# Sending the answers of the first eight expert tiles behind up to four later ones, in a routed two-layer kernel

## The chip, the core and the metric

One Trainium2 chip, one of its cores. The time is the device time of one execution in microseconds; of before there are three, and one more that was profiled. The engines are TensorE (PE), VectorE (DVE), ScalarE (ACT), GpSimd (POOL) and SyncE (SP); each works through its own instructions in order and waits for the others through semaphores.

## What is computed

Two layers over 8 x 256 tokens of width 128, each a mixing block and a feed-forward block, with a residual and a layer norm behind each. The change lies in the feed-forward block of the first layer, where each token goes to two of eight experts:

```python
scores = softmax(x2d @ gate_w.T, axis=1)
top_scores, sel = top_k(scores, 2)
# rows sorted by expert, scaled by their score
h = silu(xe @ w1[e]) * (xe @ w3[e])      # hidden width 352
out = out + h @ w2[e]                    # per expert e
out = zeros.at[token_idx].add(routed_out)
```

All of it is float32; large products are made of three passes over high and low parts.

## The kernel before

**Routing.** A first stage computes the mixing block, batch by batch. For each batch and each of its 4 columns of routed rows, GpSimd sends the rows (token, score and the place where the answer belongs) with an indirect DMA to `routed` in DRAM (`scatter`, L464 to L469), sorted by expert. The rows of batches 0 to 3 serve the first 9 expert tiles, those of 4 and 5 the next 6, the rest the last 24 (`PHASE_TILES`): 39 tiles of 128 rows (`SLOT_TILES`). The first 15 (`AHEAD`) start while the routing of the last batches still runs.

**Expert tiles.** Each tile t passes through these steps, and each engine works on several tiles at once, in a fixed order written out by hand:

- SyncE loads its 128 rows from `routed` (`load_rows`, L368 to L376), after the row transpose of tile t - 3.
- TensorE transposes them (`row_transpose`, L1782); ScalarE and VectorE make the high part (`high_row`, L740) and the low part (`low_row`, L1312).
- TensorE makes the two up products (`up_products`, L1784, matmuls at L1617 to L1619); ScalarE applies silu (`gate_row`, L746) and VectorE multiplies (`gated_row`, L1321).
- TensorE turns the hidden rows (L1806), VectorE copies them (`turned_row`, L1328), TensorE makes the down product (L1817).
- ScalarE copies the result into the tile's row buffer and counts `mo["out"]` up by one (`answer`, L752).
- GpSimd sends it with an indirect DMA of 128 rows to `answers` in DRAM (`store_answers`, L562 to L568). Where a DMA is sent by GpSimd, the instruction on GpSimd computes its descriptors and the DMA engines move the data later.

In step t ScalarE does `high_row(t)`, `gate_row(t - 1)`, `answer(t - 4)`. VectorE and TensorE have similar steps.

**Buffers.** The rows of tiles 0 to 14 have a place of their own each (`rows_ahead`), which no other tile takes. Tiles from 15 on share a ring of 11.

**GpSimd's order.** Its last scatters (batches 6 and 7) are followed at once by `store_answers(0)`, `store_answers(1)` and so on; from tile 14 on one piece of weight preparation follows each store (`prepare`, splits into high and low parts), and from tile 31 on attention work of the second layer is mixed in. The loop is:

```python
for t in range(31):
    store_answers(t)
    if t >= AHEAD - 1:
        prepare(t - AHEAD + 1)
```

**SyncE's order.** Row loads of tiles 0 to 14, among them eight writes of padding rows into `routed` (`pads`, L382); `ff_out`; 1 MB of hidden weights (`ff_h[0]`, L397); row loads from tile 15 on; between those of tile 23 and 24 a wait for `mo["stored_ahead"]` (all stores of tiles 0 to 14) and the second 1 MB (L411, L412); in the end the answers by token (`load_answers`, L405), behind waits for the stores of the later tiles.

Of the kernel before, what the change touches and what calls it, by code (L numbers as in the profile page):

```python
# [81 lines left out]
def alone(engine, carrier):  # L82

    engine.sem_inc(carrier, 1)
# [7 lines left out]
def wait(engine, semaphore, value):  # L92

    if not isinstance(value, int) or value > 0:
        engine.wait_ge(semaphore, value)

def build(nc, A, out):
# [5 lines left out]
    with ctx:  # L104
# [3 lines left out]
        def sems(prefix, names):  # L108
            return {n: ctx.enter_context(nc.semaphore(f"{prefix}_{n}")) for n in names.split()}
# [136 lines left out]
        def routed_row(t):  # L246
            return rows_ahead[:, t, :] if t < AHEAD else rows_in[:, (t - AHEAD) % RING, :]
# [73 lines left out]
        mo = sems("mo", "tr hi lo up act1 hid hid_tr hidT down out stored_ahead")  # L321
# [118 lines left out]
        def _(pool):  # L440
# [119 lines left out]
                    split_bout(n - 7)  # L560

            def store_answers(t):  # L562
                pool.wait_ge(mo["out"], t + 1)
                wait(pool, mo_out[t % FLY], 16 * ((t - AHEAD) // FLY))
                alone(pool, carrier["pool"])
                nc.gpsimd.indirect_dma_start(  # L566
                    answers[:, :], bass.IndirectOffsetOnAxis(ap=routed_row(t)[:, AT_DEST:AT_DEST + 1].bitcast(u32), axis=0),
                    routed_row(t)[:, 0:D], None).then_inc(mo["stored_ahead"] if t < AHEAD else mo_out[t % FLY], 16)  # L568
# [47 lines left out]
# [4 lines that stand above are left out]
            def attention_first():  # L620
                store_answers(31)
                answers_sum(0)
                store_answers(32)
                answers_sum(1)
                x2_root(0)
                store_answers(33)
                store_answers(34)
                x2_root(1)
                low_x2(0)
                store_answers(35)  # L630
                answers_sum(2)
                pool.wait_ge(wt["ff_lo"], 2 * FF_TILES)
                pool.memset(own_column, 0.0).then_inc(at["ones"], 1)
                pool.wait_ge(at["ones"], 1)
                for c in range(GROUP_HEADS):
                    last = pool.memset(own_column[:, c, c * HEAD_DIM:(c + 1) * HEAD_DIM], 1.0)
                last.then_inc(at["ones"], 1)
                store_answers(36)
                low_parts(0, 0)
                store_answers(37)  # L640
                low_x2(1)
                store_answers(38)
                low_parts(0, 1)
                x2_root(2)
                answers_sum(3)
                low_parts(1, 0)
                low_x2(2)
                x2_root(3)
                answers_sum(4)
# [1586 lines left out]
```

## Time and profile before

| | |
|---|---|
| median of 3 runs | 369.46 us (369.4 to 369.9) |
| the profiled execution's own time | 370.72 us |
| its span, first to last instruction | 368.9 us |
| TensorE busy | 323.3 us, 88% |
| GpSimd busy | 173.4 us, 47% |
| mean granted TensorE clock | 0.96 of full speed |
| indirect stores of answers | 39, the first at 110.2 us, the last at 200.9 us |

Times in the views below are microseconds from the span's start, taken from the profiled execution. "Clock" is the share of TensorE's full clock (2.4 GHz) that was granted; 0.50 is 1.2 GHz.

### The profile page before, as it was taken

The page shows a single profiled execution, that of the slowest core. Times are in us where ns is not written, and L with a number is a line of the kernel's source. Part 1 is how long each engine was busy: PE and PEld are TensorE (multiplying, and loading weights), DVE is VectorE, ACT ScalarE, POOL GpSimd, SP SyncE. Part 2 cuts the span into 40 slices and gives each one's busy share as a digit, 9 for nine tenths or more (in the row PEclk, how much of TensorE's full clock was granted, in tenths as well). Part 3 has the DMA queues.
Part 4 walks back from the last instruction along what each step waited for, and adds up shares of the span by engine and source line. Part 5 has one row for each costly group of instructions (what it writes and reads, how often), then busy time and mean ns, then how long its engine had stood idle before and what let it go on. Part 6 is the DMA issues. An engine that isn't in the chain of part 4 may idle for free.

```text
span 368.9 us, 8839 instructions
## 1 busy us (share of the span) xinstructions
PE 323.3 (88%) x2692; PEld 295.2 (80%) x2692; DVE 261.1 (71%) x865; ACT 210.0 (57%) x430; POOL 173.4 (47%) x237
## 2 busy tenths in 40 slices
PE   3799999976777999999985989999798999999990
PEld 1789989866676999898975778888587999999990
DVE  3558988865873567769774699987796777677841
ACT  2354777635522355455438679898366668667330
POOL 1004677763464345886478677754211342244200
PEclk9999999987985999999999899999999999999997
DMA  8990011021132533421500300000000000000001
GB/s 274 431 367 1 16 37 40 29 61 29 43 97 59 186 85 92 140 60 53 165 23 29 115 2 2 3 3 0 3 3 0 2 16 16 14 14 0 16 14 32
DMA packets 17034, 23.73 MB, mean 64 GB/s; under 512 B 3424, under 2 KB 14176, under 8 KB 16208
## 3 DMA queue, kind: packets, MB, share of 16 engines
q1 hardware_dynamic: 13712, 17.97, 15.0%
q0 software_dynamic: 2272, 4.69, 3.9%
q10 hardware_dynamic: 1008, 0.53, 0.5%
q8 instruction: 23, 0.38, 0.4%
q14 instruction: 19, 0.16, 0.1%
HBM read 17.45 MB, written 6.73 MB: 66 GB/s over the span
## 4 chain that ended last, share of the span: by engine, by line
PE 44%; issue 12%; DVE 11%; POOL 9%; ACT 3%; POOLq 0%; DVEq 0%; ACTq 0%
PE ps L1985 8%; PE ps L1986 8%; PE ps L1817 6%; PE ps L1617 5%; POOL sb_w_lo L587 4%; PE ps L1619 4%; PE ps L1618 4%; PE ps L1806 3%; PE ps L2048 3%; POOL sb_xT_lo L580 1%; DVE sb_stage L1321 1%; DVE sb_x_in L1507 1%; POOL sb_rstd_hs L454 1%; PE ps L1782 1%; POOL answers L566 1%
## 5 line engine op out<-in xcount | busy, mean ns | idle before, releaser
L1985 PE MATMUL ps<-sb_w_hi,sb_fh_hi 128*128 128x256 f32 x256 | 61.2, 283 | 1.4 <-DVE sb_w_lo L925 0.7
L1986 PE MATMUL ps<-sb_w_lo,sb_fh_hi 128*128 128x256 f32 x256 | 59.8, 278 | 0.0
L1985 PEld LDWEIGHTS ps<-sb_w_hi,sb_fh_hi 128*128 128x128 f32 x256 | 48.2, 188 | 2.5 <-issue 1.1
L1986 PEld LDWEIGHTS ps<-sb_w_lo,sb_fh_hi 128*128 128x128 f32 x256 | 48.2, 188 | 0.0
L467 POOL DMA_INDIRECT routed<-sb_rows_of,sb_row x32 | 32.1, 1003 | 16.3 <-issue 10.1
L1617 PE MATMUL ps<-sb_w_hi,sb_rT_hi 128*128 x78 | 30.4, 390 | 7.3 <-issue 5.2
L1817 PE MATMUL ps<-sb_w,sb_stage 128*128 x234 | 34.9, 288 | 0.8 <-ACT sb_stage L752 0.8
L615 POOL TENSOR_TENSOR sb_w_lo<-sb_x_in,sb_w_hi 128x256 fp32r<-128x256 f32 x24 | 17.5, 757 | 35.4 <-DVE sb_w_hi L1553 35.4
L1817 PEld LDWEIGHTS ps<-sb_w,sb_stage 128*128 128x128 f32 x234 | 31.1, 202 | 1.2 <-issue 1.0
L566 POOL DMA_INDIRECT answers<-sb_stage x24 | 24.8, 1035 | 12.8 <-issue 8.2
L587 POOL TENSOR_TENSOR sb_w_lo<-sb_x_in,sb_w_hi 128x512 fp32r<-128x512 f32 x16 | 20.7, 1295 | 16.7 <-DVE sb_w_hi L1407 16.5
L1619 PE MATMUL ps<-sb_w_hi,sb_rT_lo 128*128 x78 | 26.6, 340 | 0.0
L1618 PE MATMUL ps<-sb_w_lo,sb_rT_hi 128*128 x78 | 26.4, 338 | 0.0
L1617 PEld LDWEIGHTS ps<-sb_w_hi,sb_rT_hi 128*128 128x128 f32 x78 | 15.7, 201 | 12.0 <-issue 11.8
L1617 PE MATMUL ps<-sb_front_hi,sb_xT_hi 128*128 128x512 f32 (+1 forms) x64 | 22.8, 356 | 1.9 <-DVE sb_xT_lo L1224 1.9
L451 POOL TENSOR_TENSOR sb_veps_h<-sb_mv_h,sb_eps 128x2 f32<-128x2 f32 x16 | 4.9, 305 | 40.0 <-DVE sb_mv_h L938 34.5
L1806 PE MATMUL ps<-sb_const,sb_stage 128*128 128x128 f32 x117 | 20.3, 284 | 3.8 <-DVE sb_stage L1328 1.7
L566 POOL DMA_INDIRECT answers<-sb_xT_in x15 | 14.5, 966 | 19.1 <-ACT sb_xT_in L752 16.9
L1328 DVE COPY sb_stage<-ps 128x384 f32<-128x384 f32 x39 | 21.4, 549 | 2.3 <-remote 1.7
L746 ACT ACTIVATE sb_stage<-ps,sb_stage 128x352 f32<-128x352 f32 x24 | 13.3, 555 | 16.4 <-PE ps L1619 10.3
L849 ACT ACTIVATE sb_work<-ps,sb_ff_s 128x256 f32<-128x256 f32 x32 | 14.0, 474 | 14.9 <-PE ps L1986 14.8
L1321 DVE SCALAR_TENSOR_TENSOR sb_stage<-ps,sb_stage 128x352 f32<-128x352 f32 x24 | 14.0, 584 | 11.9 <-ACT sb_stage L746 6.5
(308 smaller groups left out, 1031.0 us busy)
## 6 DMA issues: line engine op xcount, KB each, us to landing
sb_stage<-in_w SPq DMA_DIRECT2D x2, 1408.0 KB, 13.0
sb_stage<-routed SPq DMA_DIRECT2D x24, 65.0 KB
sb_w<-in_w SPq DMA_DIRECT2D x1, 1536.0 KB, 17.5
sb_x_in<-in_x_tok SPq DMA_DIRECT2D x1, 1024.0 KB, 8.7
sb_x_in<-in_ff_h SPq DMA_DIRECT2D x1, 1024.0 KB
sb_xT_in<-in_ff_h SPq DMA_DIRECT2D x1, 1024.0 KB
sb_got_first<-answers SPq DMA_DIRECT2D x4, 256.0 KB, 3.2
sb_w<-answers SPq DMA_DIRECT2D x4, 256.0 KB, 4.5
```

Source lines behind the costliest of these rows:

```text
L467: nc.gpsimd.indirect_dma_start(routed[:, :], bass.IndirectOffsetOnAxis(ap=row[:, b, r:r + 1], axis=0), rows_of[:, b, r, :], None).then_inc ...
L566: nc.gpsimd.indirect_dma_start(answers[:, :], bass.IndirectOffsetOnAxis(ap=routed_row(t)[:, AT_DEST:AT_DEST + 1].bitcast(u32), axis=0), ro ...
L587: nc.gpsimd.tensor_tensor(st_lo[:, n, :], st[:, n, :], st_hi[:, n, :].bitcast(fp32), ALU.subtract).then_inc(at["st_lo"], 1)
L1321: V.scalar_tensor_tensor(hid[:, u % FLY, 0:HIDDEN], ps[:, 3 + u % 2, 0:HIDDEN], routed_row(u)[:, AT_SCORE:AT_SCORE + 1], act1[:, u % FLY, ...
L1328: V.tensor_copy(hidT[:, u % FLY, :], ps[:, 1, 0:HIDDEN_TILES * P]).then_inc(mo["hidT"], 1)
L1617: mm(dst, lhs[0], rhs[0], start=start, stop=False)
L1618: mm(dst, lhs[0], rhs[1], start=False, stop=False)
L1619: return mm(dst, lhs[1], rhs[0], start=False, stop=stop)
L1806: last = transpose(ps[:, 1, k * P:(k + 1) * P], hid[:, u % FLY, k * P:(k + 1) * P], ident)
L1817: last = mm(ps[:, 5, 0:D], hidT[:, u % FLY, k * P:(k + 1) * P], w2[:, e, k, :], start=k == 0, stop=k == HIDDEN_TILES - 1)
L1985: mm(dst, w_hi, x_hi, start=start, stop=False)
L1986: last = mm(dst, w_hi, x_lo, start=False, stop=stop and exact)
```

## The change

One number in one wait. `store_answers(t)` waited until answer t was written, that is until `mo["out"]` had reached t + 1. Now it waits for more answers where t is below 8: 4 more for tiles 0 and 1, 3 more for 2 and 3, 2 more for 4 and 5, 1 more for 6 and 7. From tile 8 on nothing differs.

```diff
             def store_answers(t):
-                pool.wait_ge(mo["out"], t + 1)
+                pool.wait_ge(mo["out"], t + 1 + max(0, 4 - t // 2))
                 wait(pool, mo_out[t % FLY], 16 * ((t - AHEAD) // FLY))
                 alone(pool, carrier["pool"])
                 nc.gpsimd.indirect_dma_start(
```

## Rows read from the trace of the kernel before

**Rows 1.** The page's busy time of two engines: us, share, instructions.

```profile
PE 323.3 (88%) x2692; PEld 295.2 (80%) x2692; DVE 261.1 (71%) x865; ACT 210.0 (57%) x430; POOL 173.4 (47%) x237
```

**Rows 2.** The chain that ended last, 84 to 150 us: start, length, what.

```profile
110.14 2.37 issue
...
114.64 0.65 issue
...
122.76 0.67 PE ps L1817 x6
```

**Rows 3.** GpSimd's instructions: start, length, what, idle time before and its releaser.

```profile
98.79 0.96 POOL L467 DMA_INDIRECT routed<-sb_rows_of,sb_row  x1 [4.17 <-DVE sb_rows_of L1196]
...
105.17 0.96 POOL L467 DMA_INDIRECT routed<-sb_rows_of,sb_row  x1 [1.63 <-issue]
...
110.23 0.96 POOL L566 DMA_INDIRECT answers<-sb_xT_in  x1 [0.30 <-issue]
...
112.76 0.96 POOL L566 DMA_INDIRECT answers<-sb_xT_in  x1 [0.31 <-issue]
...
133.49 0.96 POOL L566 DMA_INDIRECT answers<-sb_xT_in  x1 [1.39 <-ACT sb_xT_in L752]
...
142.49 1.00 POOL L566 DMA_INDIRECT answers<-sb_xT_in  x1 [1.43 <-ACT sb_xT_in L752]
```

**Rows 4.** ScalarE's instructions: gates 4 and 6, answers 3, 4, 5 and 10.

```profile
102.03 0.56 ACT L746 ACTIVATE sb_stage<-ps,sb_xT_in 128x352 f32<-128x352 f32 x1 [0.25 <-issue]
...
111.76 0.56 ACT L746 ACTIVATE sb_stage<-ps,sb_xT_in 128x352 f32<-128x352 f32 x1 [5.14 <-remote]
115.35 0.28 ACT L752 ACTIVATE sb_xT_in<-ps 128x128 f32<-128x128 f32 x1 [3.04 <-remote]
...
117.56 0.28 ACT L752 ACTIVATE sb_xT_in<-ps 128x128 f32<-128x128 f32 x1 [1.32 <-issue]
...
121.39 0.28 ACT L752 ACTIVATE sb_xT_in<-ps 128x128 f32<-128x128 f32 x1 [1.30 <-PE ps L1817]
...
132.43 0.28 ACT L752 ACTIVATE sb_xT_in<-ps 128x128 f32<-128x128 f32 x1 [0.44 <-PE ps L1817]
```

**Rows 5.** TensorE's instructions: transposes (L1782) of tiles 8, 10, 11, 15; up products.

```profile
101.50 0.49 PE L1619 MATMUL ps<-sb_w_hi,sb_rT_lo 128*128 x1
...
107.03 0.32 PE L1619 MATMUL ps<-sb_w_hi,sb_rT_lo 128*128 x1
...
109.87 0.27 PE L1782 MATMUL ps<-sb_const,sb_xT_in 128*128 128x128 f32 x1
112.51 0.66 PE L1617 MATMUL ps<-sb_w_hi,sb_rT_hi 128*128 x1 [2.37 <-issue]
...
121.19 0.27 PE L1782 MATMUL ps<-sb_const,sb_xT_in 128*128 128x128 f32 x1
...
123.27 0.27 PE L1782 MATMUL ps<-sb_const,sb_xT_in 128*128 128x128 f32 x1
...
132.22 0.27 PE L1782 MATMUL ps<-sb_const,sb_stage 128*128 128x128 f32 x1
```

**Rows 6.** SyncE's waits, 105 to 126 us: total, times, longest.

```profile
SPq L376 <- remote: 8.2, 1, 8.2
```

**Rows 7.** Busy time by stretch, then granted clock, DMA share and GB/s.

```profile
112.00:121.00 9.00, 7.84 (x31) 7.24 (x32) 3.65 (x8) 2.25 (x7) 3.33 (x4) 0.50 0.24 67
...
125.00:130.00 5.00, 4.89 (x38) 4.54 (x36) 2.83 (x7) 2.09 (x7) 2.40 (x3) 1.00 0.95 318
```

**Rows 8.** SyncE's instructions: a row load and the load behind the early stores.

```profile
115.54 0.33 SPq L376 DMA_DIRECT2D sb_xT_in<-routed  x1
...
144.80 0.34 SPq L412 DMA_DIRECT2D sb_xT_in<-in_ff_h  x1
```

**Rows 9.** DMA queues, 129 to 130 us: packets, MB, share of 16 engines.

```profile
q1 hardware_dynamic: 271, 0.16, 51.6%
q0 software_dynamic: 62, 0.13, 32.7%
```

## The prediction

> **What bounds the kernel now.** I began with the page: one core, TensorE busy for 88% of the span, GpSimd for 47% [rows 1]. So GpSimd's work counts only where another engine waits for it. Then I read the chain of waits around the stores that the change moves. There the expert tiles run; where they run well the chain is TensorE's matmuls, six down products in 0.67 us for example, and between 110 and 121 us it holds two issue gaps, of 2.37 and 0.65 us [rows 2]. Next come the instructions of GpSimd, ScalarE and TensorE in order of time [rows 3 to 5]. They show that the first three stores of answers (110.23 to 112.76) follow the last scatters of routed rows at a distance of 0.30 us, and that they fall in the middle of a stall. TensorE ends the up products of tile 6 at 107.35 (last matmul starts 107.03, lasts 0.32) [rows 5], yet ScalarE starts the gate of that tile at 111.76, 4.4 us later, and answer 3 at 115.35 after 3.04 us of idleness [rows 4]. The trace puts both down to a release whose source it does not show ("remote"). SyncE sees the same: it waited 8.2 us, on something just as unnamed, before the row load at 115.54, and the transpose that allows this load was recorded at 109.87 [rows 5, 6, 8]. So from 107.35 to 115.5 three engines act late on what TensorE had finished. After that TensorE's granted clock is 0.50, the 1.2 GHz level, from 112 to 121 us, and 1.00, the 2.4 GHz level, from 125 to 130 us [rows 7].
>
> **What the change does to the stores.** Nothing is added or removed: the same 39 stores, the same waits, with larger numbers in eight of them. Store t waits for answers 4, 5, 5, 6, 6, 7, 7, 8 (t = 0 to 7) in place of 0 to 7. By the answers' times of before (answer 4 starts at 117.56 and takes 0.28, so ends at 117.84; answer 5 ends at 121.67, then one about every 2.2 us to answer 10 at 132.71 [rows 4]) store 0 goes at about 117.9 in place of 110.23, store 1 at 121.7 [rows 3]. From there on GpSimd is behind: its waits are met early and it sends one store per 0.96 + 0.30 = 1.26 us [rows 3]. Store k goes at 121.7 + 1.26 x (k - 1): store 7 at 129.3, store 10 at 133.0. In the trace of before store 10 went at 133.49, once answer 10 was there [rows 3, 4]. So GpSimd has caught up by store 10, and four stores later, behind store 14 at 142.49 [rows 3], its preparation work begins as before.
>
> **Who waits for it.** Behind the waiting store on GpSimd's queue stand only further stores until store 14; then the splits of weights, which start as before. The only reader of the early stores' completion is SyncE's wait ahead of the second load of hidden weights, at 144.80 [rows 8]. It needs all fifteen, and the last of them is not moved: cost nothing. The loads of the answers themselves come behind that on the same queue. The early answers lie in a room that holds one place per early tile, so no buffer comes free later. What covers the delay is the 1.26 us pitch against a tile of 2.08 us (transposes of tiles 10 and 11 at 121.19 and 123.27 [rows 5]); if that cover were gone (stores still behind by store 14) each microsecond of lag would push the splits and the load of 144.80.
>
> **Traffic.** Two stores or so more than before fall between 124 and 130 us, where the transfer of 1 MB of hidden weights keeps the DMA engines at 0.95 [rows 7]. Two stores' packets take 32.7% of one microsecond of 16 engines, 0.33 us [rows 9]. The rows of tiles 15 and 16 land in that same microsecond, behind the 1 MB: the loads' 271 packets of 129 to 130 us [rows 9] are more than the 256 of two tiles. TensorE wants the first of them at 132.22 [rows 5]. A slack of about 2 us against 0.33 to 0.66 us (the latter if rows and stores take turns): cost nothing.
>
> **What is taken away from 110.2 to 113.7 us** is three indirect stores. The open question is whether these three have a part in the stall. Against it: the delay begins at 107.35, 2.9 us before the first of them, under scatters that stay. No engine waits for them by name. For it: the stall ends for all engines within 2 us of the last (113.72 to 115.54), and they close a row of seven indirect transfers at the 1.26 us pitch, the first at 105.17, the last at 112.76 [rows 3]. The trace does not price this, so I bound it on both sides: 0 if the stall has another source; at most the whole stall. I take 0, since the start of the stall lies ahead of anything that the change touches.
>
> The sum: 0 on GpSimd's queue, 0 in traffic, 0 from the stall. The profiled execution took 370.72 us for a span of 368.9 (1.8 us lie around it); against the median of the three runs, 369.46, it is 0.3% long. The forecast by the median stays 369.5 us.
>
> **Rivals.**
> 1. The stores help to keep the stall up, and without them it shrinks. Two sizes. If only its second half goes (answer 3 and the row load no longer late), TensorE's gap of 0.65 us goes [rows 2]: 368.8. If the first half also ends at the first moved store, 110.2 in place of 111.76, TensorE resumes 1.5 us earlier, and may keep its clock: from the up products of tile 7 (112.51) to the transpose ahead of those of tile 9 (121.19) it does two tiles in 8.7 us, the gap of 0.65 among them, while one tile at the high level took 2.08, so two 4.2 [rows 5]. That gives 1.5 + 4.5 = 6.0 us at most, 363.5; half of it, 366.5, where the clock falls anyway for part of the stretch. In favour: of the 6.0 us most is the price of a clock that follows from the stall [rows 7], so a small part of the stall taken away can bring more than itself. The Trainium skill (TensorE: Matmul & The Clock Gate, Part 1) says that the throttled level is the default and that activity releases it; the rows agree, 0.50 behind the idle stretch and 1.00 after TensorE had been busy again [rows 7].
> 2. The stall comes from a long row of indirect transfers, and the change makes a new one. Stores 1 to 10 now go every 1.26 us from 121.7 to 133 where they had pauses for each answer (1.39 us ahead of store 10 [rows 3]). It decides from the moment when such a row falls together with other loads, as it did at 105 us; at 124 to 130 us the 1 MB load is there. A second stall of the first's size costs 2.37 + 4.5 = 6.9 us; the first shrinks by up to 4.5 us at the same time. The result is 2.4 us slower, 371.9, and up to 376.4 if the old one stays whole. Against: four such transfers in a row from 98.79 on delayed nobody; the gate at 102.03 followed the last up product (101.50 + 0.49) at once [rows 3 to 5].
> 3. The waits do not move the stores (the compiler or GpSimd's order makes them late anyway): no, since stores 0 to 2 went 0.30 us behind a scatter and not behind an answer. It would give 369.5 too.
>
> **Chances.** No part in the stall, stall as before (with rival 3): 0.40, 369.5. Stall shrinks: 0.35, spread from 363.5 to 368.8, centre 366.5. New or longer stall: 0.25, 370.3 to 376.4, centre 371.9. A measurement of this kernel can tell about 0.2%, 0.7 us, from no change; a little of either rival (0.65 us and less) falls inside it, and a little of the first case falls out of it, since a stall of unknown source may move by itself when anything beside it does. So faster 0.36, same 0.38, slower 0.26. The range leaves out the largest gain and the largest loss, about 0.1 each: 365.0 to 372.5. The likeliest case's own range is 369.0 to 370.0.
>
> **What would show it.** Store 0 at about 118 us, stores 1 to 10 at a pitch of 1.26 us, store 14 and the splits where they were: the queue reading is right. Gate 6 on ScalarE still over 4 us behind the up products, and 0.50 of clock behind it: the stall is not the stores'. Wrong if the "remote" waits are gone or have become shorter (rival 1), or if new ones of that name stand between 122 and 135 us (rival 2), or if the transpose of tile 15 waits for a row load (my slack of 2 us was misread).

## The result, and the profile after

The changed kernel took 367.66 us (median of 20 executions, 363.4 to 373.24), the kernel before 369.86 beside it (20, 366.19 to 372.6). The ratio is 0.9929, with a 95% interval of 0.9901 to 0.9956: faster by 0.7%. The forecast was no change, 369.5 us, range 365.0 to 372.5. The time lies in the range; the direction was wrong.

The experiments were timed in five sessions ("call" in the texts on record), each beside the kernel before: in the first two it took about 369 us, as here, and in the last three 360 to 363, so each ratio is taken against the kernel before of its own session.

The profiled execution of after took 366.23 us for a span of 364.4; before it was 370.72 and 368.9. Not all of these 4.5 us are the change's. The first scatter of batch 6, which nothing in the change touches, starts at 98.79 in before [rows 3] and at 96.21 in after. So 2.6 us were there already, and single executions of both kernels scatter by 2 us and more around their medians. The comparison of medians, 2.2 us, is the better number for the change (the ratio makes it 2.6).

The page of after, busy time, share and instructions, against [rows 1]:

```profile
PE 320.6 (88%) x2692; PEld 291.5 (80%) x2692; DVE 261.8 (72%) x865; ACT 210.2 (58%) x430; POOL 173.5 (48%) x237
```

GpSimd does what it did, and TensorE is busy for 2.7 us less with as many matmuls: some of them ran at a higher clock. GpSimd's instructions in after, against [rows 3] (start, length, what, idle time before and who ended it):

```profile
106.38 0.96 POOL L467 DMA_INDIRECT routed<-sb_rows_of,sb_row  x1 [0.30 <-issue]
110.94 0.96 POOL L566 DMA_INDIRECT answers<-sb_xT_in  x1 [3.60 <-ACT sb_xT_in L752]
...
113.24 0.96 POOL L566 DMA_INDIRECT answers<-sb_xT_in  x1 [1.34 <-ACT sb_xT_in L752]
...
117.03 0.96 POOL L566 DMA_INDIRECT answers<-sb_xT_in  x1 [0.30 <-issue]
...
120.08 0.96 POOL L566 DMA_INDIRECT answers<-sb_xT_in  x1 [2.10 <-ACT sb_xT_in L752]
...
123.87 0.96 POOL L566 DMA_INDIRECT answers<-sb_xT_in  x1 [0.30 <-issue]
...
126.85 0.96 POOL L566 DMA_INDIRECT answers<-sb_xT_in  x1 [2.02 <-ACT sb_xT_in L752]
...
137.33 1.01 POOL L566 DMA_INDIRECT answers<-sb_xT_in  x1 [1.14 <-ACT sb_xT_in L752]
```

In before, the four scatters from 105.17 on and the first three stores made one row: seven transfers, each 1.26 us behind the one before, until 113.72. In after the four scatters stand by themselves (the last at 106.38), store 0 follows after a pause of 3.60 us, and stores 1 to 4 (113.24 to 117.03) and 5 to 8 (120.08 to 123.87) are rows of four, with pauses of 1.34 and 2.10 us ahead of them. From here on such a chain of indirect transfers at 1.26 us is called a close row; "a row of 7" is one with seven in it.

ScalarE in after, the waits that end in "remote", against [rows 4]:

```profile
101.90 0.28 ACT L752 ACTIVATE sb_xT_in<-ps 128x128 f32<-128x128 f32 x1 [2.13 <-remote]
...
117.50 0.55 ACT L746 ACTIVATE sb_stage<-ps,sb_xT_in 128x352 f32<-128x352 f32 x1 [2.66 <-remote]
119.01 0.28 ACT L752 ACTIVATE sb_xT_in<-ps 128x128 f32<-128x128 f32 x1 [0.96 <-remote]
...
125.78 0.28 ACT L752 ACTIVATE sb_xT_in<-ps 128x128 f32<-128x128 f32 x1 [2.85 <-remote]
```

The long ones of before (5.14 and 3.04 us, behind the scatters and stores of 105 to 114) are gone, and new ones stand under the two rows of stores: both rivals in part. Stretches of after, against the first line of [rows 7] (busy time of PE, PEld, DVE, ACT and POOL, then granted clock, DMA share, GB/s):

```profile
104.00:110.00 6.00, 4.58 (x33) 3.82 (x31) 4.10 (x13) 1.70 (x5) 2.73 (x3) 1.00 0.27 79
112.00:121.00 9.00, 7.36 (x51) 6.23 (x48) 4.57 (x11) 3.07 (x10) 4.75 (x5) 1.00 0.70 215
121.00:130.00 9.00, 7.29 (x52) 6.78 (x52) 3.87 (x10) 3.17 (x11) 4.84 (x6) 1.00 0.27 80
```

From 112 to 121 us before did 31 matmuls at a clock of 0.50; after does 51 at 1.00. From 121 to 130 us TensorE in after is idle for 1.7 us of 9, where in before it was hardly idle (0.1). The transposes (L1782) give the account. In before tiles 8 to 12 start theirs at 109.87, 117.3, 121.19, 123.27 and 125.3, so the steps are 7.4, 3.9, 2.1, 2.1. In after tiles 8 to 16 step by 2.4, 2.3, 2.2, 2.4, 4.2, 2.4, 3.9, 2.4. Above a pace of 2.25 us a tile, the two long steps of before lose 6.8 us and the two of after 3.6. The short steps differ as well, so the whole stretch is the better measure: from tile 8 to tile 16 before takes 24.5 us and after 22.2. The difference, 2.3 us, is of the size of the 2.2 to 2.6 that the medians show; tile 8 itself starts 2.6 us earlier, as the first scatter does. Tiles 8, 12, 13 and 16 in after, then 9 and 16 in before:

```profile
107.28 0.27 PE L1782 MATMUL ps<-sb_const,sb_xT_in 128*128 128x128 f32 x1
...
116.54 0.27 PE L1782 MATMUL ps<-sb_const,sb_xT_in 128*128 128x128 f32 x1
...
120.73 0.27 PE L1782 MATMUL ps<-sb_const,sb_xT_in 128*128 128x128 f32 x1
...
129.46 0.27 PE L1782 MATMUL ps<-sb_const,sb_stage 128*128 128x128 f32 x1
```

```profile
117.31 0.42 PE L1782 MATMUL ps<-sb_const,sb_xT_in 128*128 128x128 f32 x1
...
134.33 0.27 PE L1782 MATMUL ps<-sb_const,sb_stage 128*128 128x128 f32 x1
```

### The profile page after: what moved, and what is told of

Read it like the earlier page. It is cut to its first block, busy times and chain, and to the rows that moved or that the text cites. A ratio compares the mean times of both kernels' runs of the same rounds, so it can differ in the third digit from the quotient of the medians.

```text
span 364.4 us, 8839 instructions
## 1 busy us (share of the span) xinstructions
PE 320.6 (88%) x2692; PEld 291.5 (80%) x2692; DVE 261.8 (72%) x865; ACT 210.2 (58%) x430; POOL 173.5 (48%) x237
## 4 chain that ended last, share of the span: by engine, by line
PE 50%; DVE 13%; issue 7%; POOL 4%; ACT 3%; another core or an unknown queue 2%; DVEq 0%; POOLq 0%; ACTq 0%
PE ps L1985 9%; PE ps L1986 9%; PE ps L1617 6%; PE ps L1817 5%; PE ps L1619 5%; PE ps L1618 4%; PE ps L2048 3%; PE ps L1806 3%; POOL sb_w_lo L587 2%; PE ps L1945 1%; ACT sb_stage L746 1%; PE ps L1928 1%; DVE sb_stage L1321 1%; DVE sb_w_hi L1553 1%
## 5 line engine op out<-in xcount | busy, mean ns | idle before, releaser
L1817 PE MATMUL ps<-sb_w,sb_stage 128*128 x234 | 33.8, 281 | 2.0 <-ACT sb_xT_in L752 2.0
L1617 PE MATMUL ps<-sb_w_hi,sb_rT_hi 128*128 x78 | 29.4, 377 | 6.9 <-ACT sb_stage L746 4.1
L1817 PEld LDWEIGHTS ps<-sb_w,sb_stage 128*128 128x128 f32 x234 | 30.0, 196 | 2.7 <-issue 2.5
L1619 PE MATMUL ps<-sb_w_hi,sb_rT_lo 128*128 x78 | 25.6, 328 | 0.0
L1618 PE MATMUL ps<-sb_w_lo,sb_rT_hi 128*128 x78 | 25.5, 327 | 0.0
L1617 PEld LDWEIGHTS ps<-sb_w_hi,sb_rT_hi 128*128 128x128 f32 x78 | 14.9, 192 | 12.3 <-issue 12.1
```

The costliest lines, as they stand in the source:

```text
L1617: mm(dst, lhs[0], rhs[0], start=start, stop=False)
L1618: mm(dst, lhs[0], rhs[1], start=False, stop=False)
L1619: return mm(dst, lhs[1], rhs[0], start=False, stop=stop)
L1817: last = mm(ps[:, 5, 0:D], hidT[:, u % FLY, k * P:(k + 1) * P], w2[:, e, k, :], start=k == 0, stop=k == HIDDEN_TILES - 1)
```

## The experiments

Three theories stood at the start. A: close rows of GpSimd's indirect transfers hold back TensorE's updates until about 1 us behind the row, whatever they carry. B: only the three stores at 110 to 114 us did harm, through what they met there. C: the stall comes and goes by chance.

### First session (before: 369.17 us, median of 29 executions, a single one of 1152.91 among them)

**e1_slow_taper**: the same taper stretched over 20 stores. **e2_one_row_of_eight**: the first nine stores all wait for answer 8, which makes one long row.

```diff
-                pool.wait_ge(mo["out"], t + 1)
+                pool.wait_ge(mo["out"], t + 1 + max(0, 4 - t // 5))    # e1
+                pool.wait_ge(mo["out"], max(t + 1, 9))                 # e2
```

> Edit: the taper is slower, max(0, 4 - t // 5) in place of max(0, 4 - t // 2), so GpSimd catches up one store in five tiles and the stores never stand more than two in a row at the 1.26 us pitch. Theory A (a row of three or more indirect transfers sent one right behind the other holds back what TensorE has finished until about 1 us behind the row's end): the unnamed waits between 113 and 126 us, 2.7, 1.0 and 2.9 us in the changed kernel, are gone; those under the scatters' rows (96 to 107 us) stay; time below the changed kernel's 0.993 of before, about 0.985 to 0.990. Theory B (only the three stores at 110 to 114 us did harm, for what else moved at that time): as the changed kernel, 0.993, with unnamed waits wherever loads are. Theory C (the stall moves by chance with anything beside it): any ratio from 0.985 to 1.005, and unnamed waits that do not follow the rows.

> Edit: the first eight stores all wait until answer 8 is written, max(t + 1, 9), so that they go in one row of eight or nine at 1.26 us, about 10 us long, with no store before. Theory A: one long stall under that row, as in the kernel before (gates 3 to 5 us late, and TensorE's clock falls to 0.50 behind it); ratio 0.995 to 1.01. Theory B: the stores leave the place of harm as in the changed kernel, so 0.993 or less, and no long unnamed wait under the row.

e2 took 376.2 us (6 executions), ratio 1.0252 [1.0189, 1.0316]. GpSimd's instructions: eleven transfers stand in one row, since by the end of the ninth two more answers were ready. Then ScalarE's waits from 120 to 145 us (total, times, longest), then stretches as above:

```profile
122.09 0.96 POOL L566 DMA_INDIRECT answers<-sb_xT_in  x1 [13.29 <-ACT sb_xT_in L752]
...
134.74 0.96 POOL L566 DMA_INDIRECT answers<-sb_xT_in  x1 [0.30 <-issue]
```

```profile
ACT sb_xT_in L752 <- remote: 5.2, 1, 5.2
ACT sb_stage L746 <- remote: 4.7, 1, 4.7
...
ACT sb_rT_hi L740 <- remote: 1.1, 1, 1.1
```

```profile
122.00:129.00 7.00, 5.14 (x36) 4.27 (x34) 2.39 (x5) 1.55 (x4) 5.39 (x6) 0.99 0.23 67
129.00:142.00 13.00, 5.65 (x22) 4.78 (x21) 2.10 (x6) 2.52 (x7) 6.14 (x7) 0.50 0.16 47
```

All unnamed waits of this stretch end between 127.9 and 138 us, under the row and up to 2.2 us behind its end (135.70), and the clock is 0.50 behind them, as in before. Nothing else was moved to that place. B falls: stores do this where they stand 10 us later just as well.

e1 took 369.49 us (12), as before by the medians; the comparison gives 1.0057 [1.0017, 1.0098]. Its stores stand singly or in rows of up to 3, and its unnamed waits are short: 2.29 us under the scatters at 100.58, 0.75 under a row of 3, 0.31. Tile 15 starts at 122.4 us, some 10 us earlier than in before (132.22 [rows 5]); 4 of these were there already, as its first scatter of batch 6 starts at 94.73. But tile 24 starts at 147.7, against 152.5 in before and 147.5 in after. TensorE's waits from 140 to 155 us say where that went:

```profile
PE ps L1782 <- DMA sb_stage<-routed: 3.2, 1, 3.2
```

The row loads of tiles 24 and on stand on SyncE's queue behind the wait for the first 15 stores, and the taper makes these stores late. A gain ahead of it was given back here.

**e4_spaced_rows**: small GpSimd instructions (128x2, 0.72 us, their result is used by nobody) behind each of the last eight scatters and each of the first three stores; the waits as in before. **e6_spaced_and_taper**: the scatters spaced as in e4, and e1's taper in place of spaced stores.

```diff
+            def spacer():
+                nc.gpsimd.tensor_tensor(filler[:, next(spaces), :], eps[:, :], minus_half[:, :], ALU.pow)
...
+                    if b >= 6:        # in scatter, behind each transfer
+                        spacer()
...
+                if t < 3:             # e4 only, behind store_answers(t)
+                    spacer()
```

> Edit: the waits of the stores as in the kernel before, but behind each of the last eight scatters and of the first three stores GpSimd makes one small power of 128x2 elements (0.72 us, result unused), which opens the rows to a pitch of about 2.1 us. Theory A: no unnamed waits from 96 us on, no clock of 0.50 from 107 to 121 us; GpSimd itself is some 6 us later at the first store and has caught up by store 8 or so; ratio 0.980 to 0.990. Theory B: the stores come about 6 us later than before, so a gain like the changed kernel's, 0.993, but the unnamed waits under the scatters stay. A cost of the spacing itself could only come through the scatters landing later than tile 15's row load at 126 us; they do not.

> Edit: both, the small power behind each of the last eight scatters and the slow taper of the stores, max(0, 4 - t // 5). Theory A: no row of three anywhere behind 95 us, so no unnamed wait there; ratio 0.978 to 0.988, the best of the four. Theory B: no better than the changed kernel. Theory C: unnamed waits as often as before in other places.

In both the scatters start 1.98 us apart or so, and no unnamed wait is left under them, where before (from 107 us on), after (2.13 us at 101.90) and e1 (2.29 us) had one. In e4 (369.01 us, 12; 1.0047 [1.0004, 1.009]) GpSimd is late by the added work, and its unspaced stores make a row of 7 from 118.46 to 127.10. The stall stands there now; ScalarE's waits, 96 to 135 us:

```profile
ACT sb_xT_in L762 <- remote: 3.8, 1, 3.8
...
ACT sb_stage L756 <- remote: 2.7, 1, 2.7
```

e6 (368.41 us, 12; 0.9983 [0.9932, 1.0034]) has no unnamed wait behind 92 us at all and reaches tile 15 at 123.0 us; tile 24 starts at 147.4. SyncE's wait for the first 15 stores, 120 to 150 us, has become long, against 0.4 in after:

```profile
SPq L413 <- DMA answers<-sb_xT_in: 6.2, 1, 6.2
```

So A holds in the first session for its first half: closeness does it, and the stall goes where the rows go. But to take the rows away by a taper costs at SyncE's wait what it brings.

### Second session (before: 369.26 us, 11 executions)

**e7_taper_later_wait**: e6, with SyncE's wait for the first 15 stores and the load behind it put one group of tiles later. **e8_more_spaced_later_wait**: e7, with the four scatters of batch 5 spaced as well (`b >= 5`).

```diff
-                if t == AHEAD + 2 * FLY:
+                if t == AHEAD + 3 * FLY:
```

> Edit: e6 (small powers behind the last eight scatters, slow taper of the stores) and SyncE's wait for the first fifteen stores, with the second 1 MB load of hidden weights, one group of three tiles later (behind the row load of tile 26 in place of 23). In e6 no unnamed wait stood behind 92 us, and tile 15 was transposed at 123.0 us, 9.2 us ahead of the kernel before (4.1 ahead of the changed one), but tile 24 at 147.4, level with the changed kernel: SyncE sat behind the last early stores, and TensorE waited 3.2 us for a row load. Theory A (rows hold back TensorE's updates, and what is won goes to that wait): the 5.5 and 4.2 us steps of tiles 24 and 25 become 2.1 to 2.7, so 5 us less than e6: ratio to before 0.982 to 0.988. If it stays at e6's 0.998, the gain goes elsewhere.

> Edit: as e7, and the four scatters of batch 5 (87 to 92 us) are spaced with small powers too. Theory A: if that row of four costs anything, 1 to 3 us less than e7; by the trace of e6, which shows no unnamed wait there, the same as e7 within 0.3%.

e7 took 364.82 us (6), 0.9899 [0.9844, 0.9954]; e8 364.04 (6), 0.9873 [0.9815, 0.9932], the fastest of the study beside a before of 369. In e7 the view of waits lists for TensorE from 138 to 150 us only this one:

```profile
PE ps L1625 <- DVE sb_stage L1329: 0.4, 1, 0.4
```

Tile 24 starts at 144.8 and tile 38 at 178.7, where e6 has 147.4 and 182.5. The wait was what was late next. e8 has one unnamed wait of 2.5 us at 123.26 in a stretch with rows of 3, and one of 0.3 us at 134.12.

**e5_rows_in_mlp**: the stores and waits of before; added are close rows of 8, 2 and 4 indirect transfers of a constant to a spare place in DRAM, in steps 3, 7 and 9 of the last stage, which nobody waits for until the end. **e10_before_again**: the kernel before, profiled once more.

```diff
+                if isinstance(i, int) and i in (3, 7, 9):
+                    alone(pool, carrier["pool"])
+                    spare_row({3: 8, 7: 2, 9: 4}[i])
```

> Edit: in the last stage (dense feed-forward, no row loads, no other indirect transfer) GpSimd sends copies of a constant to a spare DRAM tensor: a row of 8 in step 3, of 2 in step 7, of 4 in step 9; steps 4 to 6 have none. Added work, no result is changed. Theory A: unnamed waits on ScalarE and VectorE (for TensorE) of 3 to 5 us under the row of 8, 1 to 3 us under that of 4, none in steps 4 to 7. Rival: the late updates need the row loads or the expert tiles' register loads as well; then GpSimd's own low parts come 10 us later in step 3, but no unnamed wait shows.

> The kernel before, unchanged, profiled once more. Theory A: the long unnamed waits stand again between 105 and 116 us, under the seven transfers in a row, since the row is the same. Theory C (chance): they are elsewhere or not there, and the row is without harm.

e5 took 378.9 us. The first and the last of the row of 8, waits from 285 to 310 us (one of VectorE's, two of ScalarE's), and three stretches:

```profile
292.19 1.03 POOL L615 DMA_INDIRECT spare<-sb_const,sb_row  x1 [0.17 <-issue]
...
301.10 0.96 POOL L615 DMA_INDIRECT spare<-sb_const,sb_row  x1 [0.30 <-issue]
```

```profile
DVE sb_work L963 <- POOL sb_rstd L456: 8.8, 1, 8.8
...
ACT sb_x_in L881 <- remote: 3.4, 2, 3.1
...
ACT sb_xT_in L872 <- remote: 2.5, 1, 2.5
```

```profile
285.00:292.00 7.00, 7.00 (x64) 7.00 (x63) 6.02 (x16) 4.15 (x8) 2.90 (x4) 1.00 0.01 2
292.00:303.00 11.00, 9.56 (x80) 9.12 (x79) 1.55 (x6) 4.31 (x9) 8.59 (x11) 1.00 0.15 49
303.00:311.00 8.00, 5.34 (x24) 4.87 (x25) 6.70 (x19) 4.39 (x8) 2.98 (x5) 0.57 0.06 16
```

TensorE was busy all the time until the row began. Under it ScalarE waits 5.9 us for matmuls that are long over, and four updates of TensorE's due between 298.4 and 299.7 us are recorded only between 303.7 and 303.9. No routed row is loaded here and no answer stored. So the transfers alone suffice, and neither routing nor the loads beside it are needed. What the stretches show beyond that is not the late signals' doing alone: VectorE waits 8.8 us for GpSimd's `sb_rstd`, which stands behind the row. f5 below has a row of 7 at the same place, no late signal, 7.4 us of the same wait, and behind the row this stretch:

```profile
295.00:303.00 8.00, 4.39 (x19) 4.10 (x20) 6.73 (x19) 1.03 (x2) 2.95 (x5) 0.65 0.06 16
```

So the 24 matmuls in 8 us at a clock of 0.57 can't be laid to late signals. Under the row of 2 one update is late by 0.2 us and no engine waits for it. Under that of 4 three are late by 0.4 to 1.2 us; it fell where TensorE was nearly done, so its cost can't be read.

e10 took 369.76 us and shows the same stall in another execution (rows of 4 and 7, the latter from 104.30 to 112.83), now with one wait of 7.3 us in place of two (the other of the two counted here, 2.0 us, stands under the row of 4); ScalarE, 96 to 130 us:

```profile
ACT sb_xT_in L752 <- remote: 9.4, 2, 7.3
```

Its tiles 8 to 10 step by 7.5 and 3.8 us, against 7.4 and 3.9 in before. C falls for these sessions: there are four executions with a row of 7 in the expert tiles (before, e4, e10, and e5, whose expert tiles are untouched), and each has unnamed waits of over 6 us under it.

### Third session (before: 360.32 us, 23 executions)

**e9_after_again**: the changed kernel. **e13_spaced_pairs**: e8's spaced scatters and later wait, no taper, a spacer behind every second of the first 15 stores. **e12_short_rows_in_mlp**: rows of 3, 5 and 4 in steps 2, 3 and 7 of the last stage. **e11_spaced_in_mlp**: 8 spaced transfers in step 3 and 8 spacers alone in step 7.

```diff
+                if t % 2 == 0 and t < AHEAD:      # e13, behind store_answers(t)
+                    spacer()
...
+                    spare_row({2: 3, 3: 5, 7: 4}[i])    # e12
...
+                if isinstance(i, int) and i == 3:       # e11
+                    alone(pool, carrier["pool"])
+                    spare_row(8, spaced=True)
+                if isinstance(i, int) and i == 7:
+                    powers(8)
```

> The changed kernel, unchanged, timed beside the others and profiled once more. Theory A: rows of four scatters, four scatters, and two rows of about four stores (113 to 125 us) with unnamed waits of 1 to 3 us under some of them, no single one of 5 us; ratio to before 0.990 to 0.996.

> Edit: as e8 (small powers behind the last twelve scatters, SyncE's wait one group later), but the stores wait for their own answer alone, as in the kernel before, and a small power stands behind every second of the first fifteen stores, so that no more than two go at the 1.26 us pitch. Theory A: the rows of three that e8 still has (one unnamed wait of 2.5 us at 123 us in it) are gone, so e8's time or up to 2 us less: ratio to before 0.980 to 0.988. It also tells whether the larger numbers in the waits have any worth of their own: by theory A none, spacing does all. If it is slower than e8 by over 0.5%, they have.

> Edit: in the last stage close rows of 3 (step 2), 5 (step 3) and 4 (step 7) indirect transfers to a spare tensor. Added work, no result is changed. Theory A: unnamed waits that grow with the row: 0 to 0.5 us under 3, 1 to 3 us under 4 and 5. If none shows under 4 or 5, the rows have to be longer when no expert tiles run.

> Edit: in the last stage GpSimd sends 8 indirect transfers to a spare tensor in step 3, with a small power behind each (pitch about 2.1 us in place of 1.26), and in step 7 a row of 8 small powers with no transfer. Added work, no result is changed. Theory A (the closeness of the transfers does it): no unnamed waits in step 3, where the close row of 8 gave 2.5 and 3.1 us, and none in step 7. Rival (the number of transfers, or their data, does it): unnamed waits in step 3 as with the close row. Rival (GpSimd's being busy without a pause does it, whatever it does): unnamed waits in step 7.

None of the four profiles has an unnamed wait, though e9 has a row of 10 (114.61 to 126.93) and e12 one of 12 (101.57 to 116.84) in the expert tiles. e9 took 360.48 us (12), ratio 0.9994 [0.9961, 1.0028]; e13 362.22 (12), 1.0026 [0.9984, 1.0067]. e12 took 365.38 and e11 378.41; of size and closeness they tell nothing, since the harm was absent from the third session. e11's 18 us above before I take to be GpSimd's own time in a stage that partly waits for it (8 transfers of 1.0 us and 16 spacers of 0.7 us, with what lies between them some 21 us); no run tests that.

Neither A as it stood nor its rivals had foreseen this. The sentence that A now needs is "in some sessions".

### Fourth and fifth session (before: 361.05 us, 29 executions; and one of 362.99)

**f3_after_2** is the changed kernel again, **f1_spaced_pairs_2** e13 and **f2_more_spaced_later_wait_2** e8. **f4_spaced_in_mlp_2** and **f6_spaced_in_mlp_3** are e11. **f5_close_then_spaced** has 7 close transfers in step 3 and 7 spaced ones in step 7:

```diff
+                if isinstance(i, int) and i in (3, 7):
+                    alone(pool, carrier["pool"])
+                    spare_row(7, spaced=i == 7)
```

> The changed kernel once more. Where rows do harm (before near 369): ratio 0.990 to 0.996, with unnamed waits of 1 to 3 us between 99 and 126 us. Where they don't (before near 360): 0.998 to 1.002, as in e9.

> The spaced pairs once more (e13). In the call of e13, e9, e11 and e12 no kernel showed a single unnamed wait, not even under close rows of 10 and 12 transfers, and the kernel before took 360.3 us there against 369.2 in the two calls before: there the rows cost nothing. So the harm of a close row depends on the chip or its state (theory A with a condition). Where it is there (before near 369): ratio 0.978 to 0.988. Where it isn't (before near 360): 1.000 to 1.006, the price of the added instructions.

> e8 once more, beside f1 and the changed kernel. Where rows do harm: 0.984 to 0.990. Where they don't: 1.000 to 1.010.

> e11 once more, since it ran where no row did harm. Where rows do harm: unnamed waits under the long close row of stores at 104 to 114 us, but none under the eight transfers spaced by small powers in step 3 of the last stage, nor under the eight small powers in step 7. If they show in step 3, it is the number of transfers and not their closeness.

> Edit: in the last stage GpSimd sends 7 close indirect transfers to a spare tensor in step 3 and 7 with a small power behind each in step 7. Added work, no result is changed. Where rows do harm (before near 369, unnamed waits at 105 to 116 us): unnamed waits in step 3, as e5 had (2.5 and 3.1 us), and none in step 7; if step 7 has them too, closeness isn't the cause. Where they don't (before near 360): no unnamed wait anywhere.

> e11 once more beside f5: 8 spaced transfers in step 3, 8 small powers without a transfer in step 7. Where rows do harm: unnamed waits at 105 to 116 us, none in the last stage. Where they don't: none anywhere, and the case of closeness against number stays open for the last stage.

Again no unnamed wait anywhere. f3 took 360.33 us (12), 0.9985 [0.9946, 1.0024]; f1 361.51 (12), 1.0004 [0.9959, 1.0049]; f2 360.43 (12), 1.0008 [0.9971, 1.0046]; f4 374.86, f5 382.45, f6 374.9. GpSimd in f3, first and last of a row of ten stores, then all of ScalarE's waits from 96 to 136 us, which are to be held against those of e2 and e10:

```profile
111.53 0.96 POOL L566 DMA_INDIRECT answers<-sb_xT_in  x1 [1.14 <-ACT sb_xT_in L752]
...
122.91 0.96 POOL L566 DMA_INDIRECT answers<-sb_xT_in  x1 [0.30 <-issue]
```

```profile
ACT sb_stage L746 <- PE ps L1619: 11.1, 15, 1.1
ACT sb_xT_in L752 <- PE ps L1817: 7.7, 13, 2.1
ACT sb_stage L752 <- PE ps L1817: 0.9, 2, 0.5
```

Every wait is for the matmul that it should be for, and none is over 2.1 us. The same code, with a longer row than the one that stopped TensorE's signals for 5 us in before, does no harm here. GpSimd's instructions last as long (0.96 us) and follow each other as closely (0.30 us) in both kinds of sessions. The one difference that the traces show is whether TensorE's updates come late. In the ten profiles of the last three sessions no recorded update of TensorE's between 60 and 340 us (over 340 in each) stands more than 0.04 us behind its matmul's end; each of the ten other profiles (before, after, and e1 to e10 without e9) has some that are late by 0.9 us and more. f5's row of 7 in the last stage was harmless too, so closeness against number could not be told apart there.

## Why the forecast was right or wrong, step by step

**Nothing added or removed; where the stores go.** The mechanism was right, the times were not. Store 0 was forecast at 117.9 us and went at 110.94, still behind answer 4. I took the answers' times from the stalled trace; with the stall shorter answer 4 came 7.7 us earlier (2.6 of them the earlier start that has nothing to do with the change), and the store follows its answer by 0.8 us, which I had left out. The one row of ten that I forecast for 121.7 to 133 became two rows of four, because answers and stores kept step. In the sessions without the harm the row of ten is there (f3).

**GpSimd has caught up by store 10; nobody waits for it.** Right. From store 9 on each waits for its answer (2.02 us ahead of the one at 126.85), store 14 goes at 137.33, 5.2 us earlier than in before, and SyncE waits 0.4 us for the first 15. I had called that wait a cost of nothing, with the condition that the last of the fifteen is not moved; e1 and e6 break the condition and pay for it, and moving the wait brought 3.6 us by medians (e6 to e7; two sessions with nearly the same before, 369.17 and 369.26).

**Traffic: nothing.** Right for the first rows: TensorE's waits from 96 to 160 us in after name no row load, neither tile 15's nor another.

**The stall: 0, since its start lies ahead of anything that the change touches.** This is the step that failed: the term was put at 0 and measured 2.2 us. Where such a stall starts does not tell how long it lasts. It started under the scatters at 105 us, which stay; it lasted until 1.7 us behind the last transfer of the row, and the last three of the row were the stores. I had this in the text as the argument "for" (all engines are released within 2 us of 113.72, and the seven stand at 1.26 us) and gave it less weight than the order of start. What I had not read were the semaphore records: they show that it is TensorE's updates alone that come late, in order, and four of the five behind the row's end (114.56 to 115.44), which points to the row's end and not to its beginning.

**Rival 1, the gain.** It came, at the low end of its span of 363.5 to 368.8: 2.2 us by the medians. Most of the price was the clock, as argued: from 112 to 121 us it is 1.00 in place of 0.50. The whole stall of before was worth 6.8 us by its two long steps, near my bound of 6.0.

**Rival 2, a new row under the stores.** It came as well, and is why the gain was small: two rows of four with waits of 2.66, 0.96 and 2.85 us, 3.6 us by their two long steps. My argument against it, that four transfers from 98.79 on delayed nobody, held for before alone: in after the same four scatters come with a wait of 2.13 us at 101.90. One trace did not show the worst of that row. What it did not bring is half clock (1.00 from 112 to 130 us).

The dose, where the harm is present, by ScalarE's and VectorE's unnamed waits under one row: a row of 2, nothing; of 3, 0 to 0.75 us and once 2.5 (e1, e8); of 4, 0 to 3.9 (before, after); of 7, 6.7 to 9.8 (before, e4, e5, e10); of 8, 5.9 (e5); of 11, 12 (e2). The waits of two engines overlap, so these sums order the rows and are not time lost. Transfers 1.98 us apart show none (e4, e6, e7). Close rows as the cause in those sessions is shown: the stall was moved (e2, e4), made anew in another stage (e5) and taken away (e6, e7). Taken away means that nothing is left which the view calls unnamed. The semaphore records are finer: rows of 2 still hold an update by up to 0.9 us (in e1 one due at 69.75 is recorded at 70.66) and rows of 3 by up to 1.9 us (e8), while under the spaced scatters none is late.

**What stays open.** What decides whether a session shows the harm: the first and the third, one of either kind, ran on a chip of the same number, so the chip alone may not be it, and the three without harm are also the last three in time. Why TensorE's updates and not VectorE's or ScalarE's: the ends of matmuls are modelled in the trace, so it can't tell whether the signal is held back or the matmul's own completion. Whether in the harmful sessions close rows explain all of the distance: e7 has no unnamed wait left and still takes 364.8 us, where the harmless sessions have 360 to 361. Part of that has a place: e7's three rows of 3 hold updates by 0.9 to 1.6 us, and from tile 8 to tile 16 it takes 19.8 us, where f3 takes 17.9. And whether spaced transfers are harmless in the last stage too, since all the runs of that (e11, f4, f5, f6) fell in sessions without harm.

**The better version.** Where close rows do harm, e8 beats the kernel before: 0.9873 [0.9815, 0.9932], where the change had 0.9929 [0.9901, 0.9956]. Whether it beats the change too is not shown: the two were not run in one session, and the intervals overlap. Where they do none, it is level (f2, 1.0008 [0.9971, 1.0046]), as the change is.

## What to carry to other kernels

When several engines act late on what TensorE had long finished, look at whose semaphore updates are late, and at what runs on GpSimd until just before they arrive: the end of a disturbance tells more than its start. Keep GpSimd's indirect transfers apart (2 us here), or at least in rows of two, which held a signal by 0.9 us at most, and when delaying them, find the first wait that counts them all and move it along. And time such a change in more than one session: what it is worth here was 0.7% in one kind and nothing in the other.

## What the runs showed of the hardware that I had not expected

- Indirect transfers issued by GpSimd every 1.26 us can make TensorE's semaphore updates late, by up to 5.3 us under a row of 7 (before, e10) and 10.2 us under a row of 11 (e2: due at 127.66, recorded at 137.91), while those of VectorE and ScalarE that are recorded in these stretches come on time. The late updates arrive in order. Some arrive inside a long row (111.73 in before, 127.87 and 131.46 in e2), the last 1 to 2.4 us after the last transfer's instruction.
- It happens in some sessions and not in others with the same code, and where it does not, the kernel before takes 360 to 363 us in place of 369.
- What a hold costs depends on the clock behind it. In before the two holds of 5.14 and 3.04 us left TensorE idle for 3.0 us but cost 6.8 us by the tiles' steps, with 0.50 of clock from 112 to 121 us; e2, with its holds close together, shows 0.50 from 129 to 142 us. In after the holds of 2.66 and 2.85 us lie 7 us apart, TensorE worked between them, and the clock stayed at 1.00. The Trainium skill (TensorE: Matmul & The Clock Gate, Part 1) calls the throttled level the default that activity releases; these rows agree.
